# A three-block tower on one core: the residual added by TensorE, both row norms measured by ScalarE, and the projection put ahead of the heads

## Chip, cores and metric

One Trainium2 chip, one core of it. The time is device time in microseconds (us), the median of three runs. One execution was also recorded by the hardware profiler; its span, from the first to the last instruction, is a little shorter than its device time.

## What is computed

The reference, cut to the shape of its three blocks (B = 64 batches, S = 16 tokens each, D = 128; 1024 rows in all):

```python
h = einsum('bg,egp->bep', x, weight * mask) + bias          # x (64, 5000), weight (16, 5000, 128)
n = layernorm(h)                                            # (x - mean) / sqrt(var + 1e-5)
cq, ckv = LN(n @ W_dq) * g + b, LN(n @ W_dkv) * g + b       # widths 64 and 85
q, k, v = 8 heads of 16 (+2 rotary) from cq, ckv and n @ W_kr
h = h + softmax(causal(q k^T / sqrt(18))) v @ W_o.T
n = layernorm(h)
h = h + shared_ffn(n) + routed_ffn(n)                       # 64 experts of width 64, top 2, capacity 256
```

## The kernel before

The 1024 rows are worked through in NCH = 8 chunks of 128 rows: chunk j holds tokens 2j and 2j + 1 of all 64 batches. Engines run written-out, in-order programs and wait for each other on counted semaphores.

Weights stream in by SyncE's queue: 48 loads of 832 KB into a ring of 12 units, two chunks deep (a unit is reloaded when its third of the chunk two before is summed), then the expert weights (w13, w2p). VectorE (`mask_pieces`, L1208) and GpSimd (`mask_pieces`, L458) multiply the units by the mask; TensorE sums over the genes in 12 steps per chunk (`sum_genes(j, n)`, L828), into bank 0.

A loop over c = 0..7 staggers three stages on each engine: chunk c is summed, chunk a = c - 1 gets its first norm, chunk b = c - 2 is projected and attends, chunk d = c - 3 gets its residual, second norm and routing. The steps that the change touches, in the order of one trip:

- `keep_h(a)` (ScalarE, L570): the sum goes from PSUM to `hres`. `stats_h(a)` (VectorE, L1292): bn_stats, bn_aggr, minus the mean, variance plus eps. `root_h` (GpSimd, L468): the power -0.5. `norm_h(a)` (ScalarE, L583) gives `xn`.
- `turn_xn(b)`, `project(b)` (TensorE): transposed and multiplied by the two down projections. `square_qk(b)` (ScalarE): both variances by Square with an accumulated sum. `root_qk` (GpSimd). `norm_qk(b)` (ScalarE), `turn_qk(b)` (TensorE), `turned_qk(b)` (ScalarE).
- `qkv(b)` (TensorE), `heads_k(b)` (ScalarE), `values(b)` (TensorE), `heads_v(b)` (ScalarE); then on VectorE `multiply_keys(b)` (L1237), `sum_scores(b)` (L1248), `less_max(b)`, ScalarE's `probs(b)`, and VectorE's `weigh_values(b)` and `sum_heads(b)` (L1282), which writes `o`.
- `turn_o(d)`, ScalarE's `copy_oT(d)`, `attend(d)` (TensorE, L902: o times W_o), `add_attended(d)` (VectorE, L1309: the residual sum and the statistics of the second norm), `root_h2(d)`, `norm_xf(d)`, `turn_xf(d)`, `copy_xfT(d)`, `gate(d)`, VectorE's `choose(d)` (top two), TensorE's `rank_tokens(d)`, VectorE's `place(d)` (slot numbers), GpSimd's `scatter` of rows into the experts' slots, in HBM.

Chunk c - 3's heads, `o(d)`, and the attention of chunk b = d + 1 are one behind the other: the attention of b begins in the same trip in which `o(d)` is used, and ends in `o(b)`, used in the next.

VectorE's trip is

```python
mask_pieces(2); add_attended(d); mask_pieces(1); mask_pieces(2)
choose(d); stats_h(a); place(d); scores(b); less_max(b)
mask_pieces(1); heads(b)
```

and GpSimd's is three mask pieces, `root_h2(d)`, `root_qk(b)`, three mask pieces, `root_h(c - 1)`, `scatter(c - 4)`. After the loop each engine has one long written-out list in which the last chunks (j, k, l = 5, 6, 7) are interleaved with the experts: eight groups of round one (tokens of chunks 0 to 4), whose slots are loaded (L398) when `scatter(4)` has landed, and four groups of round two (chunks 5 to 7). In that list TensorE comes to the first slots (`turn_xs(0)`, L978) only behind `turn_qk(6)`, `qkv(6)`, `turn_o(5)`, `values(6)`, `attend(5)` and `turn_xn(7)`.

## Time and profile before

| | |
|---|---|
| time before, median of 3 runs (lowest to highest) | 245.62 us (244.17 to 247.23) |
| profiled execution: its time / its span | 246.83 us / 245.1 us |
| busy in the span: TensorE, VectorE, ScalarE, GpSimd | 180.9, 155.1, 82.9, 146.6 us |
| mean granted TensorE clock | 0.922 of full speed |
| moved by DMA | 65.11 MB, mean 266 GB/s |

Instructions are named by line of the kernel, engine, operation and tiles (out<-in). PE is TensorE's matmul, PEld its weight load, DVE VectorE, ACT ScalarE, POOL GpSimd, SP SyncE.

### The profile page before, as it was taken

The page shows a single profiled execution, that of the slowest core. Times are in us where ns is not written, and L with a number is a line of the kernel's source. Part 1 is how long each engine was busy: PE and PEld are TensorE (multiplying, and loading weights), DVE is VectorE, ACT ScalarE, POOL GpSimd, SP SyncE. Part 2 cuts the span into 40 slices and gives each one's busy share as a digit, 9 for nine tenths or more (in the row PEclk, how much of TensorE's full clock was granted, in tenths as well). Part 3 has the DMA queues.
Part 4 walks back from the last instruction along what each step waited for, and adds up shares of the span by engine and source line. Part 5 has one row for each costly group of instructions (what it writes and reads, how often), then busy time and mean ns, then how long its engine had stood idle before and what let it go on. Part 6 is the DMA issues. An engine that isn't in the chain of part 4 may idle for free.

```text
span 245.1 us, 6074 instructions
## 1 busy us (share of the span) xinstructions
PE 180.9 (74%) x2479; PEld 148.7 (61%) x2479; DVE 155.1 (63%) x366; ACT 82.9 (34%) x245; POOL 146.6 (60%) x117
## 2 busy tenths in 40 slices
PE   0057867558989979889689589478897987999710
PEld 0056766456778868669468469256676766758410
DVE  0024187695497888988978958875799518201391
ACT  2004200003324343241341243434878651245500
POOL 3326379619998959999889688301162541276260
PEclk9999979958999999999999999655999998899985
DMA  6999999999999999999999999959401528133332
GB/s 224 278 332 419 373 414 359 385 420 415 416 414 418 427 416 421 413 418 415 419 306 217 196 207 179 137 163 272 144 3 43 144 70 259 48 99 88 108 89 55
DMA packets 32982, 65.11 MB, mean 266 GB/s; under 512 B 2875, under 2 KB 25368, under 8 KB 32376
## 3 DMA queue, kind: packets, MB, share of 16 engines
q1 hardware_dynamic: 31416, 59.47, 73.2%
q10 hardware_dynamic: 576, 3.26, 3.4%
q0 software_dynamic: 960, 1.97, 2.9%
q8 instruction: 20, 0.33, 0.6%
q14 instruction: 10, 0.07, 0.1%
HBM read 56.96 MB, written 7.73 MB: 264 GB/s over the span
## 4 chain that ended last, share of the span: by engine, by line
DMA 26%; PE 23%; DVE 21%; SPq 9%; POOL 9%; issue 6%; ACT 5%; POOLq 1%; DVEq 0%
DMA ring<-in_L_tok_weight_dram 16%; DVE ring L1224 6%; SPq L361 4%; PE bank L841 4%; DMA ring<-expert_inputs 4%; POOL ring L465 4%; DMA expert_inputs<-xf,slot_index 4%; PE bank L1004 4%; PE bank L1034 3%; DVE bank L1254 3%; DVE prod L1245 2%; POOL rstd L454 2%; SPq L367 2%; PE bank L988 2%; PE bank L978 2%
## 5 line engine op out<-in xcount | busy, mean ns | idle before, releaser
L465 POOL TENSOR_TENSOR ring<-ring,mask 128x896 f32<-128x896 f32 (+1 forms) x48 | 92.5, 1955 | 19.3 <-DMA ring<-in_L_tok_weight_dram 19.3
L841 PE MATMUL bank<-ring,xT 128*64 128x128 f32 x1248 | 81.2, 287 | 12.2 <-DVE ring L1224 8.7
L841 PEld LDWEIGHTS bank<-ring,xT 128*64 128x64 f32 x1248 | 73.4, 145 | 16.7 <-DVE ring L1224 12.7
L1224 DVE TENSOR_TENSOR ring<-ring,bank 128x1024 f32<-128x1024 f32 (+1 forms) x45 | 45.7, 1048 | 33.2 <-DMA ring<-in_L_tok_weight_dram 33.2
L454 POOL TENSOR_TENSOR rstd<-mv,half 128x1 f32<-128x1 f32 (+1 forms) x24 | 14.4, 604 | 31.8 <-DVE mv L1232 19.0
L532 POOL DMA_INDIRECT ring<-expert_outputs,slot_index x16 | 16.1, 1007 | 19.1 <-DMA expert_outputs<-ring 14.8
L507 POOL TENSOR_TENSOR mask<-ring,mask 128x256 f32<-128x256 f32 x8 | 7.5, 940 | 16.7 <-ACT ring L702 13.7
L822 PE MATMUL bank<-cst,w 64*128 64x64 f32 x39 | 5.3, 328 | 15.7 <-DMA w<-in_x_dram 15.0
L485 POOL DMA_INDIRECT expert_inputs<-xf,slot_index x14 | 14.3, 1022 | 4.1 <-issue 3.3
L1004 PE MATMUL bank<-w,ring 128*64 128x128 f32 (+1 forms) x256 | 14.2, 292 | 0.5 <-ACT ring L702 0.4
L822 PEld LDWEIGHTS bank<-cst,w 64*128 64x128 f32 x39 | 5.0, 217 | 15.9 <-issue 15.0
L1034 PE MATMUL bank<-w2p,ring 64*64 64x128 f32 (+1 forms) x256 | 13.6, 281 | 0.3 <-ACT ring L712 0.2
L1004 PEld LDWEIGHTS bank<-w,ring 128*64 128x64 f32 (+1 forms) x256 | 11.5, 133 | 2.7 <-ACT ring L693 1.1
L1034 PEld LDWEIGHTS bank<-w2p,ring 64*64 64x64 f32 (+1 forms) x256 | 10.9, 125 | 2.4 <-issue 1.5
L578 ACT ACTIVATE offset<-shift,rstd 128x1 f32<-128x1 f32 x16 | 4.7, 291 | 22.7 <-POOL rstd L454 22.7
L1254 DVE TENSOR_REDUCE bank<-prod 128x16 f32<-128x288 f32 (+7 forms) x8 | 12.1, 1511 | 0.3
L1276 DVE TENSOR_TENSOR prod<-vcat,bank 128x256 f32<-128x256 f32 (+7 forms) x8 | 10.8, 1344 | 0.0
L1284 DVE TENSOR_REDUCE bank<-prod 128x128 f32<-128x256 f32 (+7 forms) x8 | 10.6, 1321 | 0.0
L712 ACT COPY ring<-bank 128x512 f32<-128x512 f32 x12 | 7.0, 585 | 9.8 <-PE bank L1034 9.8
L1319 DVE MAX8 top<-bank 128x8 f32<-128x64 f32 x8 | 1.9, 233 | 12.7 <-PE bank L912 12.6
L1245 DVE TENSOR_TENSOR prod<-kcat,bank 128x256 f32<-128x256 f32 (+5 forms) x6 | 6.5, 1089 | 5.0 <-ACT vcat L634 5.0
L1394 DVE TENSOR_TENSOR mask<-ring,bank 128x256 f32<-128x256 f32 x4 | 1.7, 422 | 12.5 <-ACT ring L702 12.5
(151 smaller groups left out, 298.5 us busy)
## 6 DMA issues: line engine op xcount, KB each, us to landing
ring<-in_L_tok_weight_dram SPq DMA_DIRECT2D x48, 832.0 KB, 13.1
expert_inputs<-w ACTq DMA_DIRECT2D x3, 1024.0 KB, 10.2
ring<-expert_inputs SPq DMA_DIRECT2D x6, 512.0 KB, 6.5
expert_outputs<-ring SPq DMA_DIRECT2D x12, 256.0 KB, 2.6
mask<-in_L_tok_mask_dram SPq DMA_DIRECT2D x3, 832.0 KB, 15.8
w<-in_x_dram SPq DMA_DIRECT2D x1, 1250.0 KB, 13.2
w2p<-in_L_ffn_w_dram SPq DMA_DIRECT2D x1, 1024.0 KB, 19.4
xT<-masks_dram SPq DMA_DIRECT2D x1, 1024.0 KB, 8.9
```

The costliest lines, as they stand in the source:

```text
L454: pool.tensor_tensor(rstd[:, a:b], mv[:, a:b, 1], half[:, 0:b - a], ALU.pow).then_inc(s_rstd, 1)
L465: pool.tensor_tensor(unit(j, q, SPLIT(q // 2), UC), unit(j, q, SPLIT(q // 2), UC), mask[:, (m + SPLIT(q // 2)) * D:(m + UC) * D], ALU.mult ...
L485: pool.indirect_dma_start(out=xs_dram[j // NCH1], out_offset=bass.IndirectOffsetOnAxis(ap=s_idx[:, j, k:k + 1], axis=0), in_=xf[:, j, :], ...
L532: pool.indirect_dma_start(out=yg[:, 2 * j + k, :], out_offset=None, in_=ys_dram[r], in_offset=bass.IndirectOffsetOnAxis(ap=s_idx[:, j, k:k ...
L841: last = pe.matmul(bank[0][64 * par:64 * par + 64, 0:D], xT[:, (UC * t + c) * B:(UC * t + c + 1) * B], unit(j, 2 * t + par, c, c + 1), sta ...
L1004: last = pe.matmul(bank[U_BANK(g)][row:row + slots, tile * P:(tile + 1) * P], xsT[g % 2][:, n * slots:(n + 1) * slots], w13[:, EXPERT(g, n ...
L1034: last = pe.matmul(bank[Y_BANK(g)][row:row + slots, tile * D:(tile + 1) * D], hT[g % 2][H * par:H * par + H, tile * H + col:tile * H + col ...
L1224: dve.tensor_tensor(both(j, t, a, b), both(j, t, a, b), m.rearrange("p (u f) -> p u f", u=1).to_broadcast([P, 2, (b - a) * D]), ALU.mult). ...
L1245: mark(dve.tensor_tensor(pr[:, :, :, 0:DH], keys[:, :, :, 0:DH], over_keys(main, n), ALU.mult))
L1254: then(dve.tensor_reduce(raw(j).rearrange("p (h s) -> p s h", h=NH), prod[:, 0:n * f].rearrange("p (s h d) -> p s h d", h=NH, d=DK), AX.X, ...
L1276: then(dve.tensor_tensor(prod[:, 0:n * D].rearrange("p (h d s) -> p h d s", d=DH, s=n), vcat[:, :, 0:n].rearrange("p (h d) s -> p h d s", ...
L1284: then(dve.tensor_reduce(o_raw(j), prod[:, 0:n * D].rearrange("p (f s) -> p f s", f=D), AX.X, ALU.add))
```

## The change

For chunks 0 to 4 of the loop, `add_attended` leaves VectorE: `attend(d)` adds `hres` by a second matmul with the identity into the same PSUM accumulation, and ScalarE's new `keep_x(d)` copies the sum back to `hres` with an accumulated row sum. For all chunks `stats_h` leaves VectorE: `keep_h` accumulates the row sum, and the new `measure` takes the mean and, by a Square with an accumulated sum, the variance. `add_attended` stays for chunks 5, 6, 7. TensorE's trip begins with `turn_xn(b)` (before: behind the first sums) and has `project(b)` before `turn_o(d)`, `qkv(b)` before `turn_xf(d)`, `values(b)` after `gate(d)`, and `rank_tokens(d)` behind two more sums. VectorE's `multiply_keys(b)` moves to before `place(d)`. GpSimd's trip has `root_qk(b)` behind two mask pieces and `root_h2(d)` behind three.

```diff
-POOL_SHARE = (3, 3)
+POOL_SHARE = (2, 1, 3)
...
             for c in range(NCH):
                 b, d = c - 2, c - 3
                 mask_pieces(POOL_SHARE[0])
-                if d >= 0:
-                    root_h2(d)
                 if b >= 0:
                     root_qk(b)
                 mask_pieces(POOL_SHARE[1])
+                if d >= 0:
+                    root_h2(d)
+                mask_pieces(POOL_SHARE[2])
                 if c >= 1:
                     root_h(c - 1)
...
             def keep_h(j):
                 act.wait_ge(s_tok, 3 * j + 3)
-                act.copy(hres[:, j, :], bank[0][:, 0:D]).then_inc(s_hres, 1)
+                act.activation(hres[:, j, :], bank[0][:, 0:D], ACT.Identity, accum_out=row_sum[:, 0:1]).then_inc(s_hres, 1)
+
+            leans = [0]
+
+            def measure(j, i, s_var):
+
+                act.mul(shift[:, i:i + 1], row_sum[:, i:i + 1], -1.0 / D)
+                act.activation(lean[:, i:i + 1], row_sum[:, i:i + 1], ACT.Identity, bias=cst[:, C_EPS + 2:C_EPS + 3],
+                               scale=-1.0 / (D * math.sqrt(D))).then_inc(s_lean, 1)
+                leans[0] += 1
+                act.wait_ge(s_lean, leans[0])
+                act.activation(sq_wide[:], hres[:, j, :], ACT.Square, bias=lean[:, i:i + 1], scale=1.0 / math.sqrt(D),
+                               accum_out=mv[:, 3 * i, 1:2]).then_inc(s_var, 1)
+
+            def measure_h(j):
+                act.wait_ge(s_hres, j + 1)
+                if j >= 1:
+                    act.wait_ge(s_var_h, j)
+                if j >= 3:
+                    act.wait_ge(s_var_h2, min(j - 2, NCH1))
+                measure(j, 0, s_var_h)
+
+            def keep_x(j):
+                act.wait_ge(s_att, j + 1)
+                act.activation(hres[:, j, :], bank[A_BANK(j)][:, P:P + D], ACT.Identity, accum_out=row_sum[:, 1:2]).then_inc(s_summed, 1)
+                act.wait_ge(s_summed, j + 1)
+                act.wait_ge(s_var_h, j + 3)
+                measure(j, 1, s_var_h2)
...
-                if d >= 0:
-                    copy_oT(d)
                 if b >= 0:
                     copy_xnT(b)
                     square_qk(b)
                 if d >= 0:
+                    copy_oT(d)
+                if a >= 0:
+                    measure_h(a)
+                if d >= 0:
+                    keep_x(d)
+                if b >= 0:
+                    norm_qk(b)
+                    turned_qk(b)
+                if d >= 0:
                     norm_xf(d)
                 if b >= 0:
-                    norm_qk(b)
+                    heads_k(b)
                 if d >= 0:
                     copy_xfT(d)
                 if b >= 0:
-                    copy_qkv(b)
+                    heads_v(b)
...
             keep_h(l)
+            measure_h(l)
             square_qk(k)
...
             def attend(j):
                 pe.wait_ge(s_oTs, j + 1)
-                pe.matmul(bank[A_BANK(j)][:, P:P + D], oT[:], woT[:], start=True, stop=True).then_inc(s_att, 1)
+                last = pe.matmul(bank[A_BANK(j)][:, P:P + D], oT[:], woT[:], start=True, stop=j >= NCH1)
+                if j < NCH1:
+                    pe.wait_ge(s_hres, j + 1)
+                    last = pe.matmul(bank[A_BANK(j)][:, P:P + D], ident, hres[:, j, :], start=False, stop=True)
+                last.then_inc(s_att, 1)
...
                 ahead = 2 if c >= SUMS_AHEAD else 0
+                if project_b:
+                    turn_xn(b)
                 for n in range(ahead):
                     sum_genes(c, n)
+                if project_b:
+                    project(b)
                 if attend_d:
                     turn_o(d)
+                    attend(d)
+                for n in range(ahead, 3):
+                    sum_genes(c, n)
                 if project_b:
-                    turn_xn(b)
-                if attend_d:
-                    attend(d)
+                    turn_qk(b)
+                sum_genes(c, 3)
                 if project_b:
-                    project(b)
-                for n in range(ahead, 4):
-                    sum_genes(c, n)
+                    qkv(b)
                 if attend_d:
                     turn_xf(d)
-                if project_b:
-                    turn_qk(b)
                 sum_genes(c, 4)
                 if attend_d:
                     gate(d)
                 if project_b:
-                    qkv(b)
+                    values(b)
+                for n in range(5, 7):
+                    sum_genes(c, n)
                 if attend_d:
                     rank_tokens(d)
-                sum_genes(c, 5)
-                if project_b:
-                    values(b)
-                for n in range(6, 12):
+                for n in range(7, 12):
                     sum_genes(c, n)
...
                 mask_pieces(VECTOR_SHARE[0])
-                if d >= 0:
-                    add_attended(d)
...
                 if d >= 0:
                     choose(d)
-                if a >= 0:
-                    stats_h(a)
+                if b >= 0:
+                    multiply_keys(b)
                 if d >= 0:
                     place(d)
                 if b >= 0:
-                    scores(b)
+                    sum_scores(b)
                     less_max(b)
...
             weigh_values(j)
-            stats_h(l)
             weights(0, NCH1)
```

What the fence leaves out: one more constant column for the epsilon, two small tiles and two semaphores, `stats` cut to one entry, and the two helpers that nothing calls any more.

## Rows read from the trace of the kernel before

**Rows 1.** The page's part 2: granted TensorE clock and DMA share, 40 slices.

```profile
PEclk9999979958999999999999999655999998899985
DMA  6999999999999999999999999959401528133332
```

**Rows 2.** VectorE's timeline: start us, us, instruction; `o` of chunks 1, 3, 4.

```profile
86.33 0.29 DVE L1285 TENSOR_TENSOR o<-bank,mx 128x128 f32<-128x128 f32 x1
...
120.21 0.29 DVE L1285 TENSOR_TENSOR o<-bank,mx 128x128 f32<-128x128 f32 x1
...
138.78 0.29 DVE L1285 TENSOR_TENSOR o<-bank,mx 128x128 f32<-128x128 f32 x1
```

**Rows 3.** The same timeline: sum_scores of chunks 2, 4, 5.

```profile
97.96 1.06 DVE L1254 TENSOR_REDUCE bank<-prod 128x48 f32<-128x864 f32 x1
...
132.13 1.66 DVE L1254 TENSOR_REDUCE bank<-prod 128x80 f32<-128x1440 f32 x1
...
151.36 1.96 DVE L1254 TENSOR_REDUCE bank<-prod 128x96 f32<-128x1728 f32 x1
```

**Rows 4.** Timeline of all engines, trip c = 6; in brackets idle before and releaser.

```profile
121.24 0.49 PE L904 MATMUL bank<-woT,oT 128*128 128x128 f32 x2 [0.24 <-ACT oT L644]
...
122.14 0.28 DVE L1311 TENSOR_TENSOR hres<-hres,bank 128x128 f32<-128x128 f32 x1
...
122.54 0.20 ACT L598 ACTIVATION_READ_ACCUMULATOR square_junk<-bank,cst 128x1 f32 x1
...
123.13 2.94 DVE L1224 TENSOR_TENSOR ring<-ring,bank 128x1024 f32<-128x1024 f32 x3
123.30 1.24 POOL L454 TENSOR_TENSOR rstd<-mv,half 128x1 f32<-128x1 f32 x2 [1.84 <-DVE mv L1232]
123.90 0.29 ACT L578 ACTIVATE offset<-shift,rstd 128x1 f32<-128x1 f32 x1 [1.16 <-POOL rstd L454]
124.22 0.49 ACT L581 ACTIVATE xf<-hres,offset,rstd 128x128 f32<-128x128 f32 x1
124.51 5.07 POOL L465 TENSOR_TENSOR ring<-ring,mask 128x896 f32<-128x896 f32 x3
...
124.82 0.32 ACT L605 ACTIVATE qkn<-bank,rstd 128x85 f32<-128x85 f32 x1
...
125.53 1.09 PE L841 MATMUL bank<-ring,xT 128*64 128x128 f32 x16
...
126.00 0.44 ACT L619 ACTIVATE ckvT<-bank,lnp 85x128 f32<-85x128 f32 x1
...
127.03 0.23 DVE L1319 MAX8 top<-bank 128x8 f32<-128x64 f32 x1 [0.96 <-PE bank L912]
...
127.81 0.64 PE L884 MATMUL bank<-wukv,ckvT 85*64 85x128 f32 x8
...
128.58 0.38 ACT L629 COPY kcat<-bank 128x256 f32<-128x256 f32 x1
...
128.71 0.28 DVE L1328 SCALAR_TENSOR_TENSOR prod<-cst,topi,bank 128x64 f32<-128x64 f32 x1 [0.26 <-PE bank L920]
...
129.75 0.60 ACT L634 COPY vcat<-bank 128x256 f32<-128x256 f32 x1 [0.79 <-PE bank L892]
...
130.38 1.49 DVE L1245 TENSOR_TENSOR prod<-kcat,bank 128x1280 f32<-128x1280 f32 x1 [0.43 <-ACT vcat L634]
```

**Rows 5.** The chain that ended last, in order of time: start us, us, what.

```profile
152.82 7.76 DMA expert_inputs<-xf,slot_index
160.67 4.22 DMA ring<-expert_inputs
```

**Rows 6.** Timeline behind the loop: norm_qk(6) and the first slots on TensorE.

```profile
156.05 0.31 ACT L604 ACTIVATE qkn<-bank,rstd 128x64 f32<-128x64 f32 x1 [0.81 <-POOL rstd L454]
...
164.94 1.12 PE L978 MATMUL bank<-cst,ring 128*128 128x128 f32 x4 [1.02 <-DMA ring<-expert_inputs]
```

**Rows 7.** Windows: stretch, us, busy us (instructions) of each engine, PEclk, DMA share, GB/s.

```profile
160.00:162.00 2.00, 1.60 (x13) 0.97 (x11) 0.75 (x2) 1.16 (x6) 0.00 (x0) 0.50 0.05 10
```

More of the change, by code:

```diff
@@ L62 @@
 FAR = 100000.0
-C_ID, C_IOTA, C_COS, C_SIN, C_EPS, C_W = 0, 128, 192, 208, 224, 226
+C_ID, C_IOTA, C_COS, C_SIN, C_EPS, C_W = 0, 128, 192, 208, 224, 227
 C_QKV = 2 * P
@@ L155, in shape_constants @@
     c[:, C_EPS + 1] = math.sqrt(EPS / KVP)
+    c[:, C_EPS + 2] = math.sqrt(EPS / D)
     return c
@@ L210, in tower_kernel @@
         oT = sb("oT", [P, P])
-        stats = sb("stats", [P, 4, 6])
+        stats = sb("stats", [P, 6])
         warm = sb("warm", [P, 1])
+        row_sum = sb("row_sum", [P, 2])
+        lean = sb("lean", [P, 2])
         sq_junk = sb("square_junk", [P, 2, KVP])
+        sq_wide = sb("square_wide", [P, D])
         mv = sb("mv", [P, 4, 2])
@@ L306, in tower_kernel @@
         s_off = sem("norm_offset")
+        s_summed, s_lean = sem("x_kept"), sem("mean_taken")
         s_centred = sem("projections_centred")
@@ L609, in copy_xnT @@
                 act.copy(xnT[:], bank[3][:, 0:P]).then_inc(s_xnTs, 1)
-            def copy_qkv(j):
-                turned_qk(j)
-                heads_k(j)
-                heads_v(j)
             def turned_qk(j):
@@ L1228, in aggregate @@
             def aggregate(i, s_var):
-                then(dve.bn_aggr(mv[:, i, :], stats[:, i, :]))
+                then(dve.bn_aggr(mv[:, i, :], stats[:]))
                 dve.tensor_scalar(shift[:, i // 3:i // 3 + 1], mv[:, i, 0:1], -1.0, None, ALU.mult)
@@ L1257, in sum_scores @@
                 then(dve.memset(raw(j)[0:64].rearrange("p (h s) -> p h s", h=NH)[:, :, n - 1:n], NEG))
-            def scores(j):
-                multiply_keys(j)
-                sum_scores(j)
             def less_max(j):
@@ L1290, in heads @@
                 sum_heads(j)
-            def stats_h(j):
-                dve.wait_ge(s_hres, j + 1)
-                then(dve.bn_stats(stats[:, 0, :], hres[:, j, :]))
-                aggregate(0, s_var_h)
             def centre_projections():
@@ L1311, in add_attended @@
                 then(dve.tensor_tensor(hres[:, j, :], hres[:, j, :], bank[A_BANK(j)][:, P:P + D], ALU.add))
-                then(dve.bn_stats(stats[:, 3, :], hres[:, j, :]))
+                then(dve.bn_stats(stats[:], hres[:, j, :]))
                 aggregate(3, s_var_h2)
```

## The prediction

> **What bounds the kernel now.** I read the page's slices first, then the chain, then one trip of the loop on all engines, last the stretch behind the loop. DMA shows 9 of 10 or more from the second slice to the 28th but for one 5, to some 170 us [rows 1], so the weights' arrival sets the early trips; but VectorE's waits for weights end in the trip c = 4, and from there it lags behind them, so that something else sets the pace. To see what, I take `o(d)`, which ends one attention, as the zero of each trip: it ends at 86.62, 120.50 and 139.07 us [rows 2], and the next attention's `sum_scores` begins 11.34, 11.63 and 12.29 us later [rows 3]. In c = 6 VectorE sits idle three times between: 0.96 us for the gate's logits, 0.26 for the ranks, 0.43 for the values that ScalarE copies [rows 4]. Its last wait before `multiply_keys` is for `heads_v`, which ends 9.88 us after `o`. So the loop is set by a **chain of hand-overs** from `o(d)` to the keys and values of b, with VectorE not far below it. Behind the loop TensorE comes to the first expert slots 1.02 us before they land [rows 6]; they follow `scatter(4)`, whose rows take 7.76 us to land while the weight loads fill the DMA, and then 4.22 us of loading [rows 5]. Between the two DMA stands almost empty (0.05 in 160 to 162) [rows 7].
>
> **VectorE's savings.** `add_attended` runs from 122.14 to 123.13, 0.99 us [rows 4]; `stats_h` has the same four instructions behind the add, about 0.7. That is 1.7 us less in each trip. It is worth something only if what VectorE waits for comes sooner; so the chain has to be rebuilt in the new order.
>
> **The new chain, c = 6, from o(3) = 0** (all times [rows 4], unless bounded).
> - Transposing `o`, copying and the two passes with W_o end at 1.23 before (121.24 + 0.49 - 120.50). Projecting b ahead takes it off this stretch, at no gain in time, as it shared it before. The identity adds two passes; by the two of 0.49 they cost 0.2 to 0.5, say 0.3: **1.5**. The wait for `hres` is long met.
> - ScalarE is in order. Behind `copy_oT` (0.7) stands `measure_h(5)`, then `keep_x(3)`, only then `norm_qk(4)`. The price of `measure` has no row. Its two one-column steps with a wait are bounded by 0.32 (the offset step to its dependent, 123.90 to 124.22) and twice that: 0.5. Square with sum: the 128-column activation of 0.49 and the accumulator read of 0.20, at most 0.69, at least 0.4 where they overlap as the two squares of `square_qk` do; 0.55. So `measure` is **1.05** (0.75 to 1.3), and `keep_x`'s own copy with its sum 0.55 (0.4 to 0.7). measure_h ends at 1.75, the copy at 2.3, the second variance at **3.35**. Before it was there at 2.7 to 2.8: VectorE's last four were cheaper in latency.
> - GpSimd: `root_qk(4)` finds its variance early, before its second piece ends. `root_h2(3)` now has one more mask piece ahead of it (three take 5.07), but GpSimd waited 1.84 us for it, and what it gives is wanted only at 5.15. Hidden; without that cover up to 1.7 us.
> - `norm_qk(4)`: 0.52 (to 125.14), so **3.85** against 4.64. Here the early projection gains 0.8, and no more: its square and root are ready by then, but `norm_qk` stands behind `keep_x`.
> - `turn_qk` and `turned_qk` 1.30 (125.14 to 126.44): 5.15. The sums n = 2 and n = 3 lie beside this. `qkv` runs from the gate to 128.45, 1.45 to 1.5: **6.65** against 7.95.
> - Now three things stand between `qkv` and `values` that did not: `turn_xf(3)` (0.3, a short transposition), the sum n = 4 (1.09) and the gate (0.41, 126.62 to the start of choose): 8.45. Before, it was the ranks and two units' sum, which ended while ScalarE copied the keys. `heads_k` lies beside them now. `values` and `heads_v` take 1.40 (128.96 to 130.36): **9.85**, against 9.86 before. What was gained is spent.
> - VectorE: masks end at 4.75 to 4.9, then it waits for the gate until 8.45 (it had it at 6.5). `choose` 0.7, to 9.2; `multiply_keys` from 9.9 for 1.75, to 11.6. The ranks, two sums later, are there by then. `place` comes now, 1.24 (128.71 to 129.95), where it lay before `multiply_keys` and hidden in the wait for the values: **12.85** against 11.63.
>
> So a trip is 1.2 us longer in c = 6, although VectorE works 1.7 us less: its idle time grows to about 4.5 us. With the cheap prices throughout it is +0.5, with the dear ones +1.9.
>
> **The Trainium skill** (ScalarE: Activation LUTs, section on rules for kernel authors) says that adds belong on VectorE rather than ScalarE, against this change. Its section on table loads gives 186 ns + 0.833 ns per column and 93 ns more for each per-partition operand; the trace has 0.49 us for 128 columns with two of them, and the page's figures make 0.48. By it, as an estimate, a `measure` would be 1.0 with the trace's accumulator read, and a trip 0.1 shorter than mine.
>
> **Sum.** Trips c = 4, 5 and 6 give 3 x 1.15 = 3.5 (in c = 4 and before, less is put ahead on TensorE, and DMA takes up part; c = 2 and 3 I count at nothing, since the weights' arrival covers them, at +1 without that). In c = 7 `sum_scores(5)` is 0.85 later on top. The list behind the loop: `norm_qk(6)` began at 156.05, 16.98 behind `o(4)` [rows 6]. Its squares now stand behind `probs(5)`, 0.85 later, and behind keep_h's sum and `measure_h(7)`, 0.2 + 1.05: +2.1. TensorE gets to the slots that much later, less its 1.02 of waiting: +1.1. All that follows there is TensorE's and ScalarE's in-order list, so nothing gives it back. `scatter(4)`, nearly 5 us later, meets emptied queues and lands at about the same time; that hides it. Total 3.5 + 1.1 = **+4.6 us**: 251.4 against the profiled 246.83, and on the median 245.62 (1.21 lower) 250.2. Per trip bounds of +0.5 and +1.9 give +1.5 + 0.6 and +5.7 + 1.6: 247.7 and 252.9.
>
> **Rivals.**
> - *VectorE is the bound* and its saving is worth what it weighs. For it: only 1.65 us of idle in the trip of 18.57. Against it: the values wait in each trip. It decides if `heads_v` comes by about 8.2 after `o`, that is if the two measures cost half of what I take and PE passes the gate without delay. Then 3 x 1.67 = 5 us, of which the slots' side allows some 3 to 4, as the load cannot start long before the DMA empties at about 160 [rows 7]: 241.5 to 243.5.
> - *Nothing in the end*: the trip is equal within 0.3, since idle VectorE lets `choose` and `multiply_keys` start the moment that they can, and the 1.02 in front of the slots takes the rest: 245 to 246.5. Against it: `place` no longer has a wait to hide in.
> - *TensorE's clock falls*, the slower end. In the new trip TensorE waits twice where it waited less, for `norm_qk` and for the turned rows. The granted clock fell towards half (1.2 of 2.4 GHz) in two stretches in which TensorE had been waiting, near 50 us and from 155 to 172 us [rows 1], the second when it waited for `norm_qk(6)` [rows 6]; at that level the 16 passes of a four-unit sum would take up to twice their 1.09. If it happens in one trip, its sums ahead of the values add 2 to 4 us, besides the 4.6: 252 to 255. It decides if idle time gathers in one place; in the loop's slices before, the clock held at 9 throughout, so it is unlikely. (The Trainium skill, TensorE: Matmul & The Clock Gate, part 1, ties the clock to how busy the engine has lately been; the rows agree in kind.)
> - *The rows are not really ahead*: this is half of my forecast, not a rival with a time. `norm_qk` behind `keep_x` ties b's chain to `o(d)` as before.
>
> **Numbers.** Differences under 2% can't be told from no change here. The forecast has 0.60, and its 250.2 lies at +1.9%, so that about half of it is slower by over 2%; the clock 0.10; no difference 0.17; VectorE as bound 0.13, mostly within 2% or just beyond. So faster 0.11, same 0.48, slower 0.41. Range: 243.5 to 254, leaving out the better half of the VectorE case and the worse end of the clock's; the likeliest case alone is 247.5 to 253.
>
> **What would show it.** In the profile after: from `o` to `sum_scores` 12.5 to 13.2 us in c = 6 (right) or under 11.6 (wrong); VectorE's wait for the gate 3 to 4 us in each trip in place of about 1; its wait for the values near 0.6; `place` between `multiply_keys` and `sum_scores`; TensorE no longer waiting for the first slots, at 168 to 170 us; `norm_qk` within 4 us of `o`. I am wrong if ScalarE's measure is far from 1.05 us, if the passes behind `qkv` are shorter than 1.8 us, or if the early trips gain and DMA doesn't swallow it.

## The result: a tenth slower, outside the range

The changed kernel takes 272.82 us (median of 4 executions, 269.52 to 276.06), the kernel before beside it 245.93 (4 executions). The ratio is 1.100, with a 95% interval of 1.087 to 1.113. The forecast was 250.2 with a range up to 254, so it was wrong, and not by a little. The profiled execution took 274.36 us with a span of 272.6 (before 246.83 and 245.1). Executions that ran some per cent longer than the fastest of their kernel are left out of the ratios (the profiled ones of both kernels, of e3, e4 and e6 are among them), and where only one or two others remain (e3, e8, e11, e12, e14) the text gives the times of those and no ratio.

The slices of the page of the changed kernel, which answer to [rows 1]; one slice is now 6.8 us:

```profile
PEclk9999999655999959958979968995589999799995
DMA  6999999999899987894899999619900145513432
```

Before, the granted clock fell to 6 or below near 50 us, from 155 to 172 and in the last slice. Now it falls near 50 us for longer and also within the loop, to 5 near 98 and 119 us, less near 140 and 160. DMA, full until 170 us before, has gaps from 95 to 136: the weights no longer set the pace there.

The page's chain that ended last, by line, as shares of the span:

```profile
PE bank L877 14%; DMA ring<-in_L_tok_weight_dram 8%; SPq L366 4%; PE bank L1045 4%; DVE bank L1295 3%; DVE spot L1365 3%; PE bank L1075 3%; DMA ring<-expert_inputs 2%; SPq L372 2%; PE bank L928 2%; PE bank L1029 2%; PE bank L1023 2%; PE bank L920 2%; PE bank L1019 2%; PE bank L911 1%
```

The odd entry is `DVE spot L1365`, 3% of the chain: an operation on 128 x 2 elements, the first of the three small ones that end `place`. Two idle times of the same page are long as well: GpSimd waits 58.2 us in all ahead of the roots, VectorE 34.7 ahead of the gate's logits.

The timeline of the changed kernel (start us, us, engine, line, instruction; in brackets the idle time before and its releaser). The rows of L1322 are `o` of chunks 1, 3 and 4 and answer to [rows 2]; those from 141.86 to 159.09 are the trip c = 6, as [rows 4] and the second of [rows 3]:

```profile
47.58 4.27 POOL L470 TENSOR_TENSOR ring<-ring,mask 128x896 f32<-128x896 f32 x2 [1.16 <-DMA ring<-in_L_tok_weight_dram]
47.76 2.15 DVE L1242 TENSOR_TENSOR prod<-rope_in,cst 64x128 f32<-64x128 f32 x1
49.95 2.04 DVE L1244 TENSOR_TENSOR wqr<-wqr,sc 64x128 f32<-64x128 f32 x1
...
87.45 4.15 POOL L470 TENSOR_TENSOR ring<-ring,mask 128x896 f32<-128x896 f32 x2
...
88.86 0.71 DVE L1365 SCALAR_TENSOR_TENSOR spot<-topi,rank 128x2 f32<-128x2 uint32 x1
89.49 2.13 DVE L1366 TENSOR_SCALAR spot<-rank 128x2 f32<-128x2 f32 x1
...
95.73 0.29 DVE L1322 TENSOR_TENSOR o<-bank,mx 128x128 f32<-128x128 f32 x1
...
108.37 4.16 POOL L470 TENSOR_TENSOR ring<-ring,mask 128x896 f32<-128x896 f32 x2
108.68 0.27 DVE L1360 SCALAR_TENSOR_TENSOR prod<-cst,topi,bank 128x64 f32<-128x64 f32 x1
...
109.20 3.36 DVE L1365 SCALAR_TENSOR_TENSOR spot<-topi,rank 128x2 f32<-128x2 uint32 x1
112.48 0.16 DVE L1366 TENSOR_SCALAR spot<-rank 128x2 f32<-128x2 f32 x1
...
141.86 0.29 DVE L1322 TENSOR_TENSOR o<-bank,mx 128x128 f32<-128x128 f32 x1
...
144.33 0.19 ACT L589 ACTIVATION_READ_ACCUMULATOR square_wide<-hres,lean 128x1 f32 x1
...
145.63 0.19 ACT L589 ACTIVATION_READ_ACCUMULATOR square_wide<-hres,lean 128x1 f32 x1
...
145.92 0.32 ACT L638 ACTIVATE qkn<-bank,rstd 128x85 f32<-128x85 f32 x1
...
150.81 0.23 DVE L1351 MAX8 top<-bank 128x8 f32<-128x64 f32 x1 [4.08 <-PE bank L952]
...
152.04 1.49 DVE L1286 TENSOR_TENSOR prod<-kcat,bank 128x1280 f32<-128x1280 f32 x1 [0.47 <-ACT vcat L662]
...
154.01 0.98 POOL L490 DMA_INDIRECT expert_inputs<-xf,slot_index  x1 [0.30 <-issue]
...
154.19 0.16 DVE L1365 SCALAR_TENSOR_TENSOR spot<-topi,rank 128x2 f32<-128x2 uint32 x1
154.27 0.16 DVE L1366 TENSOR_SCALAR spot<-rank 128x2 f32<-128x2 f32 x1
154.47 4.70 DVE L1368 TENSOR_TENSOR slot_index<-spot 128x2 uint32<-128x2 f32 x1
154.99 4.14 POOL L470 TENSOR_TENSOR ring<-ring,mask 128x896 f32<-128x896 f32 x2
...
159.09 1.65 DVE L1295 TENSOR_REDUCE bank<-prod 128x80 f32<-128x1440 f32 x1
...
165.72 0.29 DVE L1322 TENSOR_TENSOR o<-bank,mx 128x128 f32<-128x128 f32 x1
```

Where the time went: `o(0)` ends at 75.55 us (before 71.18), so 4.4 us are lost up to there. The four trips that follow take 20.47, 21.90, 24.23 and 23.86 us, from `o` to `o`, where they took 15.44, 16.51, 17.37 and 18.57: 5.0, 5.4, 6.9 and 5.3 us more. The fifth, c = 7, takes 20.92 for 21.22, and behind it less than 1 us is added. So 27 us come from the loop.

In c = 6 the forecast chain comes out at `multiply_keys` (9.89 us behind `o`, forecast 9.9), though not step by step. Then `place` begins, and its last instruction, on 128 x 2 elements, takes 4.70 us. It starts 0.52 us before GpSimd's two mask pieces, beside the last instruction of the scatter (`DMA_INDIRECT`), and ends at 159.17; the pieces end at 159.13. In c = 4 the first of the three takes 3.36 and ends at 112.56; GpSimd's pieces end at 112.53. The same is seen in c = 5 (4.24 us). In c = 3 it has another form: the first operation (0.71 us) ends as the first of the two pieces does, and the second (2.13) is held over the other piece. L1360, which reads the ranks from PSUM, ran at 108.68 beside the same pieces and took its normal 0.27. In c = 7, where GpSimd has no pieces left, the three take 0.74 together; one of them takes 0.42 and ends as an instruction of the scatter does, so mask pieces are not all that holds. Before, `place` ran just as GpSimd's batch came to its end (124.51 + 5.07 in [rows 4]); the timeline of the kernel before:

```profile
129.24 0.36 DVE L1333 SCALAR_TENSOR_TENSOR spot<-topi,rank 128x2 f32<-128x2 uint32 x1
129.53 0.23 DVE L1334 TENSOR_SCALAR spot<-rank 128x2 f32<-128x2 f32 x1
129.79 0.16 DVE L1336 TENSOR_TENSOR slot_index<-spot 128x2 uint32<-128x2 f32 x1
```

The same holds the second half of `turn_rope` near 48 us: two of its products take 2.15 and 2.04 us in place of 0.28, ending just behind GpSimd's pieces. GpSimd is early there, because the first norm's root no longer waits for VectorE: `root_h(0)` starts at 45.79 us, before at 54.39.

**Theory 1**, then: an instruction of VectorE that has its data in SBUF is held while GpSimd's mask pieces run, and the change moved `place` from the end of a batch of them to where the next trip's batch begins. **Theory 2**: the measuring on ScalarE and TensorE's new order are dearer than I thought, and the clock, which falls in the waits, doubles that; the long `place` is a by-product.

### The profile page after: what moved, and what is told of

Its sections match the earlier page's. It is cut to its first block, busy times and chain, and to the rows that moved or that the text cites. A ratio compares the mean times of both kernels' runs of the same rounds, so it can differ in the third digit from the quotient of the medians.

```text
span 272.6 us, 6119 instructions
## 1 busy us (share of the span) xinstructions
PE 195.6 (72%) x2489; PEld 159.0 (58%) x2489; DVE 159.2 (58%) x309; ACT 95.4 (35%) x315; POOL 146.0 (54%) x117
## 3 DMA queue, kind: packets, MB, share of 16 engines
q0 software_dynamic: 960, 1.97, 2.4%
## 4 chain that ended last, share of the span: by engine, by line
PE 39%; DVE 17%; DMA 13%; ACT 10%; issue 9%; SPq 8%; POOL 2%; POOLq 1%; ACTq 0%; DVEq 0%
PE bank L877 14%; DMA ring<-in_L_tok_weight_dram 8%; SPq L366 4%; PE bank L1045 4%; DVE bank L1295 3%; DVE spot L1365 3%; PE bank L1075 3%; DMA ring<-expert_inputs 2%; SPq L372 2%; PE bank L928 2%; PE bank L1029 2%; PE bank L1023 2%; PE bank L920 2%; PE bank L1019 2%; PE bank L911 1%
## 5 line engine op out<-in xcount | busy, mean ns | idle before, releaser
L877 PE MATMUL bank<-ring,xT 128*64 128x128 f32 x1248 | 90.0, 304 | 14.2 <-DVE ring L1265 11.7
L877 PEld LDWEIGHTS bank<-ring,xT 128*64 128x64 f32 x1248 | 79.7, 155 | 20.3 <-DVE ring L1265 13.1
L1265 DVE TENSOR_TENSOR ring<-ring,bank 128x1024 f32<-128x1024 f32 (+1 forms) x45 | 45.0, 1048 | 31.2 <-DMA ring<-in_L_tok_weight_dram 31.2
L459 POOL TENSOR_TENSOR rstd<-mv,half 128x1 f32<-128x1 f32 (+1 forms) x24 | 14.4, 604 | 58.2 <-ACT square_junk L631 56.2
L1351 DVE MAX8 top<-bank 128x8 f32<-128x64 f32 x8 | 1.9, 232 | 34.7 <-PE bank L952 34.7
L490 POOL DMA_INDIRECT expert_inputs<-xf,slot_index x14 | 14.3, 1021 | 4.8 <-issue 3.0
L895 PE MATMUL bank<-cst,qkn 128*128 128x128 f32 x8 | 3.3, 417 | 15.6 <-ACT qkn L614 14.9
L668 ACT ACTIVATE bank<-sc 128x16 f32<-128x16 f32 (+7 forms) x8 | 1.9, 236 | 33.2 <-DVE sc L1304 33.2
L1075 PEld LDWEIGHTS bank<-w2p,ring 64*64 64x64 f32 (+1 forms) x256 | 10.9, 125 | 2.4 <-issue 1.5
L895 PEld LDWEIGHTS bank<-cst,qkn 128*128 128x128 f32 x8 | 1.3, 166 | 17.4 <-ACT qkn L614 15.9
```

The costliest lines, as they stand in the source:

```text
L459: pool.tensor_tensor(rstd[:, a:b], mv[:, a:b, 1], half[:, 0:b - a], ALU.pow).then_inc(s_rstd, 1)
L490: pool.indirect_dma_start(out=xs_dram[j // NCH1], out_offset=bass.IndirectOffsetOnAxis(ap=s_idx[:, j, k:k + 1], axis=0), in_=xf[:, j, :], ...
L877: last = pe.matmul(bank[0][64 * par:64 * par + 64, 0:D], xT[:, (UC * t + c) * B:(UC * t + c + 1) * B], unit(j, 2 * t + par, c, c + 1), sta ...
L1075: last = pe.matmul(bank[Y_BANK(g)][row:row + slots, tile * D:(tile + 1) * D], hT[g % 2][H * par:H * par + H, tile * H + col:tile * H + col ...
L1265: dve.tensor_tensor(both(j, t, a, b), both(j, t, a, b), m.rearrange("p (u f) -> p u f", u=1).to_broadcast([P, 2, (b - a) * D]), ALU.mult). ...
```

## Experiments

Line numbers in the rows shift by a few with each edit; the operations are the same.

**e1, e2 and e3: take away what holds VectorE.** In e1 the ranks and one of the two spot tiles lie in PSUM, in unused columns of the chunk's own bank, for chunks 0 to 4:

```diff
+rk = bank[A_BANK(j)][:, 100:102] if j < NCH1 else rank[:]
+sp = bank[A_BANK(j)][:, 104:108].rearrange("p (a b) -> p a b", a=2) if j < NCH1 else spot[:]
...
-mark(dve.scalar_tensor_tensor(spot[:, 0, :], topi[:, j, 0:2], slots, rank[:], ALU.mult, ALU.add))
-mark(dve.tensor_scalar(spot[:, 1, :], rank[:], 0.5 - slots, FAR, ALU.add, ALU.mult))
+mark(dve.scalar_tensor_tensor(spot[:, 0, :], topi[:, j, 0:2], slots, rk, ALU.mult, ALU.add))
+mark(dve.tensor_scalar(sp[:, 1, :], rk, 0.5 - slots, FAR, ALU.add, ALU.mult))
...
-dve.tensor_tensor(where, spot[:, 0, :], spot[:, 1, :], ALU.max).then_inc(s_slot, 1)
+dve.tensor_tensor(where, spot[:, 0, :], sp[:, 1, :], ALU.max).then_inc(s_slot, 1)
```

> The changed kernel, but place() of chunks 0 to 4 keeps the rank and one of the two candidate slots in PSUM, so that none of its small VectorE instructions reads two SBUF operands. Theory 1 (they wait until GpSimd's mask pieces end, because both read SBUF through something shared): each of the three takes about 0.16 us, trips c = 3 to 6 shorten by the 2.5, 3.2, 4.1 and 4.5 us that the trace shows in them, 14 us in all: 258 to 261 us. Theory 2 (the order alone: the gate is late and place lies in no wait): nothing changes, 270 to 275. Theory 3 (TensorE's clock): the same 270 to 275, as nothing of TensorE is touched.

Measured: 252.0 us (249.61 to 254.56) against 243.04, ratio 1.034 (1.022 to 1.047). The timeline of e1, c = 4:

```profile
105.09 4.17 POOL L470 TENSOR_TENSOR ring<-ring,mask 128x896 f32<-128x896 f32 x2
...
105.65 0.16 DVE L1367 SCALAR_TENSOR_TENSOR spot<-topi,bank 128x2 f32<-128x2 uint32 x1
105.73 0.16 DVE L1368 TENSOR_SCALAR bank<-bank 128x2 f32<-128x2 f32 x1
105.92 0.16 DVE L1370 TENSOR_TENSOR slot_index<-spot,bank 128x2 uint32<-128x2 f32 x1
106.00 1.06 DVE L1295 TENSOR_REDUCE bank<-prod 128x48 f32<-128x864 f32 x1
```

GpSimd's pieces run under the same three instructions as in c = 4 of the changed kernel, and these take 0.16 us each. Two thirds of the loss are gone, by the ratios some 16 us, a little more than the holds' own 14. The time lies 6 us below the 258 to 261 that theory 1 gave, and 3 of these are that the kernel before took 243.04 beside it and not 245.93. The trips take 19.64, 18.31, 17.78 and 18.51 us: the last two as before the change (17.37 and 18.57), the first two still 4.2 and 1.8 longer.

In e2 GpSimd waits at the start of trip c = 2 for the rotation, and nothing else is changed:

```diff
+if c == 2:
+    pool.wait_ge(s_rope, 2)
 mask_pieces(POOL_SHARE[0])
```

> The changed kernel, but GpSimd waits at the head of trip c = 2 until VectorE has turned the rotary weights. Theory 1: the two instructions of turn_rope that took 2.15 and 2.04 us take 0.3, the sums of chunk 1 come some 3.8 us sooner, TensorE idles less before them; 266 to 270 us. Theory 2: o(0) is late because of the order of roots and sums, so 270 to 275 and o(0) still near 75.5 us.

Measured: 264.59 us, ratio 1.089 (1.077 to 1.100). The rotation is no longer held, yet `o(0)` ends at 75.39, as late as in the changed kernel (75.55). The timeline of e2 says why:

```profile
49.14 4.10 POOL L470 TENSOR_TENSOR ring<-ring,mask 128x896 f32<-128x896 f32 x2 [2.21 <-DVE wqr L1247]
...
49.63 3.67 DVE L1341 TENSOR_SCALAR wproj<-wproj,mx 128x64 f32<-128x64 f32 x2
```

The wait only pushed the pieces onto the next steps of VectorE: the two that centre the projections take 3.67 us for 0.43. What little e2 may gain (its interval overlaps that of the changed kernel) comes from later trips, in which `place` missed the pieces or met less of them (0.16 us in c = 5, 2.17 in c = 6). So the expectation for `o(0)` failed, and e9 mends the edit.

e3 has both edits.

> The two edits together (operands of place in PSUM, rotary weights before GpSimd's pieces). Theory 1: the effects add, 18 us: 253 to 257 us; what is left above the kernel before is the 1.2 us a trip that the order costs, and the clock. Theory 2: 270 to 275.

Measured: 249.04 us, less than the 253 to 257 expected. It is no better than e9 below and decides nothing by itself.

**e4: the move alone, in the kernel before.** All of the change is left out but one: VectorE multiplies the keys ahead of `place`.

```diff
+if b >= 0:
+    multiply_keys(b)
 if d >= 0:
     place(d)
 if b >= 0:
-    scores(b)
+    sum_scores(b)
```

> The kernel before with one part of the change: VectorE's multiply_keys stands ahead of place; nothing else. Theory 1: place's last three instructions now fall on or just before GpSimd's three mask pieces that follow the scatter (6.2 us): a trip loses 1.2 us for the lost cover and up to 6 more, 255 to 270 us. Theory 2: 1.2 us a trip, 250 to 251 us.

Measured: 270.5 us, ratio 1.109 (1.101 to 1.117). This one move, without any measuring on ScalarE and with TensorE's old order, gives the whole loss of the change. Timeline of e4, c = 4:

```profile
103.97 6.20 DVE L1333 SCALAR_TENSOR_TENSOR spot<-topi,rank 128x2 f32<-128x2 uint32 x1
103.98 6.16 POOL L465 TENSOR_TENSOR ring<-ring,mask 128x896 f32<-128x896 f32 x3
110.09 0.15 DVE L1334 TENSOR_SCALAR spot<-rank 128x2 f32<-128x2 f32 x1
```

Here GpSimd has three pieces in a row, and VectorE is held over all three, not only to the end of the first: 6.20 us.

**e6 and e7: the same in PSUM.** e6 is the kernel before with e1's edit, e7 is e4 with it.

> The kernel before with the rank and one of the two spot tiles in PSUM for the first six chunks, nothing else. Theory 1: in the kernel before place meets only the end of GpSimd's pieces (0.34 to 0.42 us in place of 0.16), so at most 1 us is won: 242 to 243.5 us against 243.0. Rival: PSUM operands make the small operations cheaper by themselves, whatever GpSimd does; then it wins nothing more than that either, but the 0.16 us of the operations that weren't held falls too.

> The kernel before with multiply_keys ahead of place (which took 270.5 us) and with rank and one spot tile in PSUM. Theory 1 (the port): place's operations fall back to 0.16 us and the time returns to 243 to 247 us. Rival (the order itself puts something late, the slot behind the product): it stays above 258 us although the operations are short.

e6 measured 245.1 us against 245.71, ratio 0.999 (0.993 to 1.004): the kernel before loses nothing worth measuring at `place`. e7 measured 248.76, ratio 1.020 (1.008 to 1.032): of the 10.9% that e4 loses 2.0 are left, with VectorE's order as in e4 and 0.16 us for each of the small operations up to the trip c = 7. The expectation (up to 247) was a little low: the order itself, with the product ahead of the slots, costs 0.8 to 3.2% by the interval.

**e5: put `place` back in its place.** The changed kernel with one move on VectorE:

```diff
-if b >= 0:
-    multiply_keys(b)
 if d >= 0:
     place(d)
 if b >= 0:
+    multiply_keys(b)
     sum_scores(b)
```

> The changed kernel with one thing put back: on VectorE place(d) stands ahead of multiply_keys(b) again. Theory 1 (place's small operations, which read two tiles of SBUF, are held by GpSimd's mask pieces): place now comes 1.2 to 2 us earlier in the trip and mostly before the pieces, so its operations take 0.16 to 0.5 us in at least three of the five trips and the time is 246 to 256 us. Theory 2 (the loss comes from what the change lengthens on the chain: the measuring on ScalarE and TensorE's new order): place's order is worth nothing, 262 us or more.

Measured: 270.71 us, ratio 1.109 (1.096 to 1.123). By the number, theory 2; but the experiment didn't do what I wanted. Timeline of e5, c = 4:

```profile
108.30 0.28 DVE L1360 SCALAR_TENSOR_TENSOR prod<-cst,topi,bank 128x64 f32<-128x64 f32 x1 [1.31 <-PE bank L960]
...
108.83 4.10 DVE L1365 SCALAR_TENSOR_TENSOR spot<-topi,rank 128x2 f32<-128x2 uint32 x1
```

The ranks stand behind two more batches of sums in TensorE's new order, so that VectorE now waits 1.31 us for them, about as long as it multiplied before. `place` begins at 108.30 (in the changed kernel at 108.68), the same pieces hold it, and in c = 3 and 6 as well (0.70 and 2.13, 4.79). My premise that it would come 1.2 to 2 us earlier was false, so its time tells the theories apart in no way. Its trips speak for theory 1: c = 5, in which `place` missed the pieces (0.16 us for each operation), takes 20.07 us, and c = 4 and 6, in which it was held, take 22.89 and 25.23. The run also shows that TensorE's order puts `place` there as much as VectorE's does.

**e11: let the pieces wait for `place`.** Nothing in PSUM, VectorE's order as in the changed kernel:

```diff
+if c >= 4:
+    pool.wait_ge(s_slot, c - 3)
 mask_pieces(POOL_SHARE[0])
```

> The changed kernel as it is, but GpSimd waits before each trip's first mask pieces (c >= 4) until the last trip's place is done; nothing in PSUM, VectorE's order untouched. Theory 1 (the pieces hold place): no operation of place above 0.5 us behind c = 3, GpSimd waits 1 to 3 us a trip, the time is 250 to 258 us. Rival (place is slow for a reason of its own, the pieces' end is chance): place keeps its 3 to 5 us and the added waits come on top, over 272 us.

Measured: 249.54 and 250.00 us against 243.56, that is 2.5% over the kernel before where the changed kernel is 10.0% over it, and all by adding a wait. Timeline of e11, c = 4:

```profile
105.42 0.16 DVE L1367 SCALAR_TENSOR_TENSOR spot<-topi,rank 128x2 f32<-128x2 uint32 x1
105.49 0.16 DVE L1368 TENSOR_SCALAR spot<-rank 128x2 f32<-128x2 f32 x1
105.69 0.16 DVE L1370 TENSOR_TENSOR slot_index<-spot 128x2 uint32<-128x2 f32 x1
...
105.94 4.14 POOL L470 TENSOR_TENSOR ring<-ring,mask 128x896 f32<-128x896 f32 x2 [1.01 <-DVE slot_index L1370]
```

GpSimd gives 1.01 us, VectorE gets back more than 3. The operands are in SBUF as in the changed kernel, so it isn't PSUM that makes the operations short; with e4 and e1 this settles the cause of the large part.

**e9 and e10: what is left beside the kernel before.** e9 is e1 with GpSimd waiting at c = 2 until the projections are centred. e10 is e9 with TensorE turning the rows behind two batches of sums in the trips c < 5. Both edits, e9's first:

```diff
+if c == 2:
+    pool.wait_ge(s_centred, 2)
 mask_pieces(POOL_SHARE[0])
...
-for n in range(ahead, 3):
+early = 3 if c >= SUMS_AHEAD else 2
+for n in range(ahead, early):
     sum_genes(c, n)
 if project_b:
     turn_qk(b)
-sum_genes(c, 3)
+for n in range(early, 4):
+    sum_genes(c, n)
```

> e1 (place's rank and spot in PSUM) and GpSimd waits at the start of trip c = 2 until VectorE has centred the projections (in e2 it waited for the rotation alone, and its pieces then held the centring, 3.67 us for 0.43). Theory 1: the first o, 2.3 us late in e1, comes at 70.5 to 71.5 us, and the total falls by 1.5 to 2.5 us to 249.5 to 250.5. Rival: the first o is late by the measuring and the new order, and stays at 73 us: 252.

> e9 and TensorE turns the rows behind two batches of sums, not three, in the trips c < 5. In e1's trip c = 3 these three batches (40 passes, 3.92 us at the lower clock) held turn_qk 2.3 us. Theory 1: trip c = 3 falls from 19.6 to 17.5 to 18.5 us, and the total by 1 to 2 us below e9. Rival: the batches are only moved behind the rows, TensorE is as full as before, and the total is e9's within 0.5 us.

e9 measured 249.47 against 243.56, ratio 1.025 (1.017 to 1.033); `o(0)` ends at 71.88 us, and c = 3 takes 18.02. e10 measured 247.83, ratio 1.015 (1.008 to 1.023); `o(0)` ends at 69.79, c = 3 takes 18.29. By the medians the early hold is worth some 2 us and the batch another 1.6. The intervals overlap, so the trips have to carry this: `o(0)` comes 1.3 us earlier in e9 than in e1 and c = 3 is 1.6 shorter; in e10 `o(0)` comes 2.1 earlier still, but c = 3, where I expected the gain, is 0.3 longer.

**e14: the old order in c = 3.** e10 with `turn_o` and `copy_oT` first in that trip, and ScalarE's DMA issues behind the values:

```diff
+if c == 3:
+    copy_oT(d)
 if b >= 0:
     copy_xnT(b)
     square_qk(b)
-if d >= 0:
+if c > 3:
     copy_oT(d)
...
+if c == 3:
+    turn_o(d)
 if project_b:
     turn_xn(b)
...
+if c == 3:
+    attend(d)
 if project_b:
     project(b)
-if attend_d:
+if c > 3:
     turn_o(d)
     attend(d)
```

> e10 with the old order for trip c = 3 alone (turn_o and copy_oT ahead of the rows of chunk 1) and ScalarE's DMA issues moved from the start of trips c = 3 and 5 behind the values. In e10's trip c = 3 the first o is at 69.8 us and its transpose only starts at 71.9, behind the row's projection and 0.8 us of DMA issues on ScalarE. Theory 1: this trip falls from 18.3 to 16.5 to 17.5 us and the total to 246 to 247 us. Rival: the trip is bound by TensorE's sums, not by o's chain: 247.5 to 248.5 us as e10.

Measured: 244.81 and 247.62 us against 244.10; c = 3 takes 17.84 in the profiled one, 0.45 less than in e10 and not the 0.8 to 1.8 expected. The total may be e10's or 1 to 2 us below. No kernel of this study beats the one before by an amount that can be told.

**e8, e12 and e13: the measuring alone.** In e8 TensorE adds the residual and ScalarE measures both norms, as in the change, and all else of the order is the old one (`place` first, TensorE's and GpSimd's old lists). e12 is e8 with e1's edit; e13 is e12 with the fifth batch of sums ahead of `turn_xf`. In short, e8 against the changed kernel and, behind the last line of dots, e13 against e12:

```diff
-POOL_SHARE = (2, 1, 3)
+POOL_SHARE = (3, 3)
...
+if d >= 0:
+    copy_oT(d)
 if b >= 0:
     copy_xnT(b)
     square_qk(b)
-if d >= 0:
-    copy_oT(d)
 if a >= 0:
     measure_h(a)
 if d >= 0:
     keep_x(d)
-if b >= 0:
-    norm_qk(b)
-    turned_qk(b)
-if d >= 0:
     norm_xf(d)
+if b >= 0:
+    norm_qk(b)
...
+sum_genes(c, 4)
 if attend_d:
     turn_xf(d)
 if project_b:
     turn_qk(b)
-sum_genes(c, 4)
```

> Only the parts that give the change its name: TensorE adds the residual, ScalarE takes both means and variances; the order of TensorE, GpSimd, VectorE and the rest of ScalarE as in the kernel before. Theory 1: without the move of multiply_keys there is no long stall at place; the measuring (about 0.9 us) with the first norm's ahead of the second's costs 1 to 2 us a trip in three trips: 246 to 252 us. Rival (VectorE bounds the trips, and it is relieved of about 2 us a chunk): 239 to 242 us. Second rival (the measuring itself is the loss): over 258 us.

> e8 (residual on TensorE and measuring on ScalarE alone, all orders as in the kernel before) with rank and one spot tile in PSUM. Theory 1: in e8's profiled run no operation of place was held over 0.45 us, so what it loses in trips c = 3 to 6 (1.4 to 3.1 us each) is the measuring's own place on the chain, and e12 takes 256 to 261 us. Rival (the port costs e8 as well, in the runs that took up to 271 us): 248 to 254 us and a narrower spread.

> e12 with one line moved on TensorE: the fifth batch of sums (16 passes) stands ahead of turn_xf and turn_qk. In e12 TensorE waited 2.63 us for the normed rows in trip c = 6, then the granted clock fell to 1.2 GHz and the following 80 sums took 6.06 us for 4.54. Theory 1 (the wait's length is paid a second time by the clock): with the wait half filled the clock holds, trips c = 6 and 7 fall from 23.5 and 24.8 to below 21.5, the time is 250 to 258 us. Rival (only the chain's length counts): the batch delays the gate by up to 1.1 us, and the time is 264 us or more.

e8: 259.68 and 261.81 us. e12: 260.04 and 262.07. e13: median 263.06, ratio 1.073 (1.062 to 1.084). So the measuring without the new orders costs 14 to 18.5 us. For e8 that is the second rival, not my theory 1. None of it is `place`, whose small operations take 0.16 us up to c = 7 in e12; and e8, without PSUM, takes the same time. But not all of it need be the measuring: the early hold is here too, and longer. VectorE's timeline of e12:

```profile
47.81 2.15 DVE L1238 TENSOR_TENSOR prod<-rope_in,cst 64x128 f32<-64x128 f32 x1
50.00 2.04 DVE L1240 TENSOR_TENSOR wqr<-wqr,sc 64x128 f32<-64x128 f32 x1
51.97 2.15 DVE L1241 TENSOR_TENSOR wqr<-wqr,prod 64x128 f32<-64x128 f32 x1
```

Three products of the rotation take 6.3 us for 0.8, in e8 as in e12, and `o(0)` ends at 76.24 and 75.16 us, 5.1 and 4.0 later than before the change. No run takes this hold out of e8 or e12, so how much of their loss it causes isn't settled. Timeline and one window (stretch, us, busy us and count of each engine, granted clock, DMA share, GB/s) of e12, c = 6:

```profile
129.40 0.29 DVE L1318 TENSOR_TENSOR o<-bank,mx 128x128 f32<-128x128 f32 x1
...
131.44 0.31 ACT L630 ACTIVATE square_junk<-bank,cst 128x64 f32<-128x64 f32 x1 [0.89 <-PE bank L896]
...
132.86 0.26 ACT L601 ACTIVATE hres<-bank 128x128 f32<-128x128 f32 x1
...
135.16 0.49 ACT L613 ACTIVATE xf<-hres,offset,rstd 128x128 f32<-128x128 f32 x1
...
135.71 0.33 PE L945 MATMUL bank<-cst,xf 128*128 128x128 f32 x1 [2.63 <-ACT xf L613]
...
136.47 1.97 PE L874 MATMUL bank<-ring,xT 128*64 128x128 f32 x16
...
143.60 6.06 PE L874 MATMUL bank<-ring,xT 128*64 128x128 f32 x80
```

```profile
136.10:146.40 10.30, 10.27 (x90) 8.99 (x92) 3.54 (x14) 2.10 (x6) 9.80 (x8) 0.52 1.04 219
```

`xf` ends 5.96 us behind `o`, before 4.21 ([rows 4]): ScalarE squares the projections and measures the first norm before it comes to `keep_x`. That is 1.75 us. TensorE, which waited 2.63 us for `xf`, then runs with a granted clock of 0.52, about 1.2 GHz: 16 passes take 1.97 us for 1.09 [rows 4]. The trip is 4.9 us longer than before; 1.75 of that is the chain, and passes at the lower clock may be most of the rest. In e13 1.76 us of the wait are left, and the trips c = 6 and 7 fall from 23.49 and 24.83 to 20.76 and 22.59; but c = 5 rises from 19.09 to 20.91, `o(0)` comes 4 us later, and the total is unchanged. I expected 250 to 258, so this failed, and how much of e12's loss is the clock stays open.

## Why the prediction was wrong

**The step that failed** is the last of the new chain: "`place` comes now, 1.24 [...], where it lay before `multiply_keys` and hidden in the wait for the values: 12.85". The sum up to it comes out (`multiply_keys` at 9.89 for 9.9; gate at 8.66 for 8.45; `measure` 0.93 for 1.05, from 143.59 to 144.52), in part by luck: `square_qk` still lay ahead of `copy_oT` behind `o`, so that `attend` ends 2.32 us behind `o` for 1.5, the second variance comes at 3.67 for 3.35 and `norm_qk` at 4.09 for 3.85; the steps from `qkv` to the values were shorter than priced and made up for it. But the price of `place` was read from the kernel before, where the three small operations just met the end of GpSimd's pieces; that 0.36 stood there in place of 0.16 was the sign of it. I moved them by 3 us without asking what GpSimd does at the new time. What it does is the next trip's mask pieces, 4.2 us without a gap, and `place` is held until they end: 2.5, 3.2, 4.1 and 4.5 us more than their normal time in c = 3 to 6, 14.3 in all. The rest comes behind it. `o` is late, GpSimd waits 7.8 us for the next squares, and then the gap between its scatter and its next pieces comes at the same point of the next trip: each hold sets up the next. TensorE, having waited, does its next sums at the lower clock (16 passes 1.98 us at 121.62). That is how I read the trace; what the runs show is that e1 and e11, which take away the hold of `place` alone, get back 6.6 and 7.5 of the 10.0%, and that e4, which moves `place` into the pieces and changes nothing else, loses 10.9, of which 2.0 are left when the hold is taken away (e7).

The rule that I left out stands in the Trainium skill, SBUF — State Buffer, section "Who interferes with whom". It says that a VectorE instruction with two inputs in SBUF contends with a GpSimd instruction that reads SBUF, and that whichever issues first has the shared ports for the whole instruction while the other "fully blocks". The rows agree (3.36 us for 0.16, and 0.16 again with one operand in PSUM), and the operation with a single SBUF tile was held too (2.13 us, L1366, c = 3), as the section says a tensor_scalar may be in some of its modes. The section speaks of one instruction; here VectorE stayed blocked over two and three in a row in the trips c = 4 to 6, but not in c = 3.

**The early trips.** "c = 2 and 3 I count at nothing, since the weights' arrival covers them, at +1 without that". Wrong as well, and a second instance of the same oversight: `root_h(0)`, early by 8.6 us, starts GpSimd's pieces beside `turn_rope` (e9: some 2 us). The rest in c = 3 and 4 (4.2 and 1.8 us in e1) may in part be `turn_qk` behind three batches (e10: 1.6 by the medians). Of the 1.5% that e10 still loses, what is the measuring and what TensorE's order isn't settled.

**Trips c = 5 and 6.** With the hold away, they take 17.78 and 18.51 us in e1, +0.4 and -0.1 where I had +1.15. In e1's c = 6 the gate comes 7.8 us behind `o` and `sum_scores` 11.57 (before 11.63, forecast 12.85): the row's projection is done before `o` and its squares as `o` ends (129.04 against 128.95), so the rows are ahead by more than I allowed. And e12 beside e1 shows what the new orders are good for: with them e1 takes some 9 us less (7.2% over the kernel before in e12, 3.4 in e1). Some 2 of these stand at `o(0)` already, where e12's rotation is held over one more piece; the rest may be measuring that the new orders hide.

**Behind the loop** I had +1.1 us; it is less than 1, with TensorE no longer waiting for the first slots, as forecast.

**The rivals.** VectorE as the bound: no; its wait for the gate is 4.1 to 6.2 us in each trip. The clock: it did fall in the loop, which I called unlikely, in c = 5 and 6 as a follower of the holds: without them it stayed at 1.00 in the trips c = 5 and 6 (in c = 3 and 4 of e1 it was 0.91, so it fell there without them too), as the windows of e1 show:

```profile
111.00:129.00 18.00, 15.09 (x208) 12.22 (x208) 13.56 (x30) 8.16 (x35) 15.04 (x11) 1.00 0.98 362
129.00:147.50 18.50, 14.90 (x207) 12.08 (x207) 14.52 (x29) 7.64 (x32) 15.46 (x12) 1.00 1.03 266
```

Its price was right in kind (16 passes at nearly twice the time). The rule for adds in the Trainium skill, ScalarE: Activation LUTs, section "Rules for kernel authors", which the forecast quotes, didn't decide it: a `measure` took 0.93 us, near the estimate of 1.0, and in e1 two trips hide it.

## What to carry to other kernels

Before an instruction of VectorE is moved, read what GpSimd does at the new time: a tiny operation cost 0.16 us here or as much as GpSimd's whole batch, up to 6.2 us, and only GpSimd's rows tell which. An operation that ends at the very moment at which another engine's batch ends, a little longer than its twins elsewhere, is the sign that it was held there already. Where such an operation can't be moved away, one operand in PSUM, or one wait that lets it go first, is the cure; then ask which operation the other engine falls upon next (e2).

## What the hardware did that I had not expected

- VectorE's block can outlast a GpSimd instruction: 6.20 us over three pieces (e4), 4.1 to 4.8 over two. That was so in the trips in which a scatter stands ahead of the pieces. In c = 2 and 3, which have none, each held operation ended with a piece and the next was held over the following one (2.15 and 2.04 us; 0.71 and 2.13; in c = 3 of e4 0.32, 2.12 and 1.98). Whether the scatter makes the difference no run tests.
- A scatter instruction held as well: in c = 7 an operation beside it took 0.42 us for 0.16 and ended with it (178.55 against 178.56), while the one before it, beside the same scatter, took its normal 0.16.
- An operation on one SBUF tile with constants is held as well: 2.13 us for 0.16 (c = 3). So are the two that centre the projections, whose second operand is one value per row, also in SBUF: 3.67 us for 0.43 (e2).
- With one of its two tiles in PSUM, the same operation beside the same pieces takes 0.16 us (e1), and VectorE's own mask products, which read one tile from PSUM, take their normal 1.21 beside them (e1, 107.59).
- A wait of 2.63 us on TensorE was followed by 10 us at a granted clock of 0.52 (e12), in which 80 passes took 6.06 us.
